# Second attention: the float8 stage's quantised rows transposed by DMA from SBUF to SBUF, in place of TensorE and ScalarE

## The reference

```python
x = x + _L1_xattn_ref(_layernorm(x), ctx_1024, ctx_1024, fside_BxSxS2_0, ...)   # 16 heads of 16, bias fside * lambda
x = x + _L1_ffn_ref(_layernorm(x), L1_ffn_weight, L1_ffn_bias)

def _L1_ffn_ref(x, weight, bias):
    x_mat = quantize_e4m3(x2d, SCALE).astype(jnp.float16)    # clip to 448, round to float8
    w_mat = quantize_e4m3(weight, SCALE).astype(jnp.float16)
    out2d = (x_mat @ w_mat.T).astype(jnp.float32)
    return (out2d + bias)
```

## Time and profile before

| | |
|---|---|
| time, median of 3 runs (lowest, highest) | 1896.82 us (1893.7, 1897.35) |
| profiled execution: its own time, its span | 1893.5 us, 1891.7 us |
| granted TensorE clock, mean over the span | 0.975 of full |
| PE, DVE, ACT, POOL busy over the span | 89%, 63%, 59%, 36% |
| last phase in the span | 1469.9 to 1891.7 us |
| one steady turn of it | 24.7 us |

### The profile page before, as it was taken

How to read it: one execution, slowest core, us unless ns; L and a number is a source line. 1 busy time by engine, 2 the same in 40 slices (tenths; PEclk the granted TensorE clock), 3 DMA queues, 4 the chain that set the end, 5 groups by cost and what they waited for, 6 DMA issues and landing times. The chain is left out here.

```text
span 1891.7 us, 40735 instructions
## 1 busy us (share of the span) xinstructions
PE 1683.7 (89%) x13412; PEld 1382.6 (73%) x13412; DVE 1187.3 (63%) x4106; ACT 1117.7 (59%) x2571; POOL 683.4 (36%) x857
## 2 busy tenths in 40 slices
PE   6777777769999999999997899989999899999995
PEld 5555555557788888888996777777778677777774
DVE  6799999857301101011113899999985798888885
ACT  5599999942222222222334665666664788888894
POOL 4423232321211111110104466656654244445544
PEclk9899999979999999999998999999999899999998
DMA  3100010025855655655985200000000201111110
GB/s 131 49 19 27 19 27 19 3 79 187 274 174 176 201 178 169 202 178 161 332 270 168 73 23 20 15 23 23 23 29 1 74 23 34 35 36 35 36 63 29
DMA packets 111696, 171.96 MB, mean 91 GB/s; under 512 B 6832, under 2 KB 86576, under 8 KB 110864
## 3 DMA queue, kind: packets, MB, share of 16 engines
q1 hardware_dynamic: 95248, 142.55, 23.1%
q0 software_dynamic: 6480, 17.70, 3.2%
q10 hardware_dynamic: 9776, 9.31, 1.4%
HBM read 143.45 MB, written 26.08 MB: 90 GB/s over the span
## 5 line engine op out<-in xcount | busy, mean ns | idle before, releaser
L2151 ACT ACTIVATE moe_hT<-moe_p_h,lane_a 128x256 f32<-128x256 f32 (+1 forms) x344 | 131.4, 433 | 370.7 <-PE moe_p_h L2093 370.7
L2093 PE MATMUL moe_p_h<-moe_gT,moe_w 128*128 128x256 f32 (+1 forms) x1376 | 256.4, 345 | 0.8 <-issue 0.8
L2103 PE MATMUL moe_p_y<-moe_w,moe_hT 128*128 128x256 f32 x1136 | 252.3, 379 | 0.0
L2093 PEld LDWEIGHTS moe_p_h<-moe_gT,moe_w 128*128 128x128 f32 x1376 | 227.8, 192 | 25.8 <-issue 1.2
L1584 ACT ACTIVATE xb_pr<-xb_sc,xb_nmax 128x256 f32<-128x256 f32 x512 | 222.7, 503 | 29.9 <-DVE xb_nmax L1667 28.2
L1983 POOL DMA_INDIRECT moe_gx<-moe_tokens,moe_source_i x71 | 67.4, 949 | 457.5 <-PE moe_p_t L2080 401.5
L2103 PEld LDWEIGHTS moe_p_y<-moe_w,moe_hT 128*128 128x128 f32 x1136 | 212.5, 190 | 27.1
L999 ACT ACTIVATE xa_pr<-xa_sc,xa_nmax 128x256 f32<-128x256 f32 (+1 forms) x512 | 204.0, 452 | 21.3 <-DVE xa_nmax L1079 20.5
L1667 DVE CUSTOM_DVE_ANT_0 xb_sc<-xb_p_s,begun_area 128x256 f32<-128x256 f32 x512 | 187.1, 419 | 41.0 <-PE xb_p_s L1415 39.4
L2271 DVE COPY moe_gT<-moe_p_t 128x512 f32<-128x512 f32 (+1 forms) x43 | 25.7, 599 | 233.2 <-PE moe_p_t L2080 226.8
L2296 DVE TENSOR_TENSOR moe_gy<-moe_p_y,lane_a 128x256 f32<-128x256 f32 x71 | 27.6, 421 | 229.0 <-PE moe_p_y L2103 229.0
(11 more groups left out here) (376 smaller groups left out, 3442.1 us busy)
## 6 DMA issues: line engine op xcount, KB each, us to landing
moe_w<-in_L_ffn_w_dram SPq DMA_DIRECT2D x86, 1024.0 KB
begun_area<-xb_kv SPq DMA_DIRECT2D x32, 256.0 KB, 2.8
moe_rows_out<-moe_gy ACTq DMA_DIRECT2D x28, 256.0 KB
xb_kv<-moe_w SPq DMA_DIRECT2D x18, 256.0 KB, 4.9
X<-in_x_dram SPq DMA_DIRECT2D x4, 1024.0 KB, 9.5
xa_ctx<-in_ctx_turned_dram SPq DMA_DIRECT2D x16, 256.0 KB, 9.8
moe_tokens<-moe_XN_s SPq DMA_DIRECT2D x16, 256.0 KB, 2.3
xb_raw<-in_fside_BxSxS_dram SPq DMA_DIRECT2D x15, 256.0 KB, 3.7
```

Source lines behind the costliest of these rows:

```text
L2093: last = pe.matmul(p_h[n % 3][:, k * width:(k + 1) * width], w1[:, r, ic, (2 * n + k) * P:(2 * n + k + 1) * P], gT[:, r % 2, ic, 0:width], ...
L2103: last = pe.matmul(p_y[:, t * D:(t + 1) * D], hT[:, hc, t * P:(t + 1) * P], w2[:, r, hc, :], start=(hc == 0), stop=(hc == HC - 1))
L2151: last = act.activation(hT[:, 2 * n + k, 0:width], p_h[n % 3][:, k * width:(k + 1) * width], ACT.Gelu, bias=b1[:, bass.ds(e * HC + 2 * n + ...
```

## The change

The bf16 transposes of f_xq leave PE, and the copy of p_a to f_xT leaves ACT. SP issues two DMAs with transpose instead, from f_xq straight to f_xT, one for each tile of 128 rows (64 KB each), in its iteration b for batch b - 2; for batches 14 and 15 after its loop and ahead of the stores. They count on a semaphore of their own, f_xT_in, for which PE's product waits, and for which the writers of the single f_xq wait. The identity's bf16 copy goes, and with it PE's wait for it.

```diff
@@ block.sync
+            def turn_float8(f):
+                sp.wait_ge(s_["f_quantised"], f + 1)
+                if f >= 1:
+                    sp.wait_ge(s_["f_y_ready"], f)
+                for t in range(TB):
+                    sp.dma_start(f_xT[:, :, t * P:(t + 1) * P], f_xq[:, t, :], transpose=True).then_inc(f_xT_in, 16)
+
             for b, h, s in turns(sp):
                 if has_next(b):
...
                     load(b + 1, h + s, 1 - s)
+                if b >= 2:
+                    turn_float8(b - 2)
+            turn_float8(B - 2)
+            turn_float8(B - 1)
             out_v = out.rearrange("b (t p) d -> p (b t) d", p=P)
@@ block.gpsimd
-            pool.tensor_copy(ident_b[:, :], ident[:, :]).then_inc(s_["ident_set"], 1)
...
-                    wait_alone(pool, s_["stood_p"], (s_["f_turned"], f))
+                    wait_alone(pool, s_["stood_p"], (f_xT_in, 16 * TB * f))
@@ block.tensor
-            def turn_float8(f):
-                pe.wait_ge(s_["f_quantised"], f + 1)
-                for c in range(DC):
-                    for t in range(TB):
-                        last = pe.transpose(p_ab[:, c * S + t * P:c * S + (t + 1) * P], f_xq[:, t, c * P:(c + 1) * P], ident_b[:, :])
-                last.then_inc(s_["f_turned"], 1)
...
-                pe.wait_ge(s_["f_x_ready"], f + 1)
+                pe.wait_ge(f_xT_in, 16 * TB * (f + 1))
...
-            pe.wait_ge(s_["ident_set"], 1)
...
-                    if g == 1 and b >= 3:
-                        pe.wait_ge(s_["o_ready"], TB * (b - 1) + 1)
-                        turn_float8(b - 3)
...
                     if g == 1 and b >= 3:
+                        pe.wait_ge(s_["o_ready"], TB * (b - 1) + 1)
                         multiply_float8(b - 3)
...
-                turn_float8(f)
                 multiply_float8(f)
@@ block.scalar
-            def read_float8(f):
-                act.wait_ge(s_["f_turned"], f + 1)
-                if f >= 1:
-                    act.wait_ge(s_["f_y_ready"], f)
-                act.activation(flat(f_xT[:, :, :]), p_ab, ACT.Copy).then_inc(s_["f_x_ready"], 1)
...
-                    if g == 1 and b >= 3:
-                        read_float8(b - 3)
...
-                read_float8(f)
                 read_float8_product(f)
@@ block.vector
-                wait_alone(dve, s_["stood_v"], (s_["f_turned"], f))
+                wait_alone(dve, s_["stood_v"], (f_xT_in, 16 * TB * f))
```

More of the change, by code:

```diff
@@ L1186, in biased_attention_and_float8 @@
         wt_ffn = sh.wt_ffn
-        ident_b = ph.sb("ident_b", [P, P], BF16)
         f_stats = ph.sb("f_stats", [P, TB, 6])
@@ L1215, in biased_attention_and_float8 @@
         p_a = ph.ps("p_a")
-        p_ab = p_a[:, :].bitcast(BF16)[:, 0:512]
         p_s = [ph.ps(f"p_s{i}") for i in range(4)]
@@ L1223, in biased_attention_and_float8 @@
                  "pv sums_read sums_turned o_ready turned_o oT_ready y_ready y_biased added chain_v chain_p stood_v stood_p "
-                 "ident_set f_measured f_var f_rooted f_normed f_cast f_quantised f_turned f_x_ready f_y_ready f_y_read "
+                 "f_measured f_var f_rooted f_normed f_cast f_quantised f_y_ready f_y_read "
                  "f_biased f_added f_last stored").split()
@@ L1228, in biased_attention_and_float8 @@
         raw_in = [ph.sem(f"raw_in{s}") for s in range(2)]
+        f_xT_in = ph.sem("f_xT_in")
         block = ph.block()
```

## The result

| | before | after |
|---|---|---|
| median of six runs each (lowest, highest) | 1895.82 us (1893.49, 1897.35) | 1903.01 us (1900.94, 1906.51) |
| profiled execution: its time, its span | 1893.5, 1891.7 us | 1901.87, 1900.1 us |
| granted clock, mean | 0.975 | 0.972 |

The ratio is 1.0041, 95% interval 1.0027 to 1.0054: slower by 7.2 us between the medians, 5 to 10 by the interval. The place, the sign and the mechanism were as predicted; the loss was forecast at 11.3 us.

What follows compares the result with a forecast made beforehand. Steady turns bound by a path through DVE, ACT, PE, DVE, unaffected; end: 1883.85 + 0.14 + 3.1 + 11.5 + 3.8 + 1.0 - 0.4 = 1903.0 us span, 1904.8 profiled, 1908.1 us for the median, range 1902 to 1920.

Steps and rivals of the forecast that it cites:

- inner range of 1902 to 1912: Own range of the likeliest forecast, 1908.1 us, chance 0.72: bounds of the pair's time and 3.7 us between runs.
- The bound and the hidden work: Steady turns, 24.7 us: path DVE, ACT, PE, DVE; removed 0.40 on PE and 0.60 on ACT lie beside it, gain 0.
- Rivals A and D: Steady turns shorter: first up to 1.0 us each, 1891.8, chance 0.02; second 0.5 to 0.8, 1897 to 1901, 0.06.
- The start: At phase start, without POOL's identity copy and PE's wait for it, first scores come 0.4 us earlier, kept to the end.
- I take 3.1 us: Time the two transposing DMAs of a batch hold SP and its queue; bounds 0.8 to 6.4 us.
- Rivals B and C: Pair holds SP over 12.1 us, turns grow, 1944 at 14, chance 0.10; second 6.4 to 12.1, 1911 to 1917, 0.10.
- The ring and its threshold (12.1 us): Quantise, transposes, loads, POOL keys, quantise: closes in pair time + 3.6 + 8.95 us, so under 12.1 the turn stays 24.7.
- The stores: At the end: all four behind SP's last pair, big store issued 1887.1 not 1810.34, landing 11.5, others 3.8 us more.
- I take 0: PE's four transposes a batch, 0.40 us: removal gains nothing, hidden by two units turned behind; at most 0.40 a turn.

Runs made afterwards that it cites:

- e7: Before without float8 transposes, copies or DMAs in their place; the product reads an f_xT filled once, PE doesn't wait at its first scores: 1892.37 us, one run.
- e3: Before with PE's wait for the identity moved from its first scores to its first float8 transposes: 1898.77 us, one run.
- e1: After with stores earlier in SP's order, batches 0 to 10 ahead of batch 12's pair, 11 and 12 ahead of batch 14's: 1895.42 us, ratio 1.0011 to before.
- e4: e1 with transposes and copies of batches 14 and 15 back on PE and ACT: 1893.74 us, ratio 0.9993.
- e5: e1 with transposes and copies of batches 13 to 15 back on PE and ACT: 1896.74 us, ratio 1.0006.
- e6: After with three or five spare transpose pairs ahead of each true one, batches 0 to 13: 1902.22 us with four pairs, 1964.11 with six, one run each.
- e2: Before, no DMA transposes, with SP waiting for the last quantised rows ahead of its stores: 1904.74 us, ratio 1.0052.

## Why the prediction was right, and where it was off

The forecast was 1908.1 us, range 1902 to 1920, and slower with 0.92; it came out at 1903.0, in the range, near its lower end. Of the 5.1 us between, 1.0 is the base: the median of before was 1896.82 over three runs and 1895.82 over six. The inner range of 1902 to 1912 takes the 3.7 us of the runs' spread off at its lower end and doesn't add it at the upper, which would be 1915; no verdict hangs on that. By its steps:

- **The bound and the hidden work: right for the steady turn.** 24.68 us in after, ACT idle 1.53 us (forecast about 1.5), and turns 0 to 15 take 390.0 to 390.2 us in three profiles of before and three of after alike. e7 shows that even no turning at all leaves it. Rivals A and D fall.
- **The start: right.** First scores 0.04 us behind SP's first issue in after, 0.46 before; e3 shows 0.41 us. In after the first scores also took 1.23 us against 2.09, at a granted clock of 0.86 against 0.50; the other two profiles of after have 2.09 and 1.44, so this is chance in part. Of the other kernels that do not wait for the identity, e1, e3, e4, e5 and e7 had 2.09 and the two of e6 1.50 and 1.91; the four profiles that wait (before three times, e2) all had 2.09.
- **"I take 3.1 us" for the pair: 2.5 measured.** The bounds (0.8, 6.4) held it. The row that I doubled, the longest issue of 1.56 us, was an outlier; one transposing DMA holds SP for 1.24, three times a plain issue of 0.43. Rivals B and C fall. A landing is counted from the start of its issue, so the pair had landed 1.29 + 0.04 + 2.39 = 3.72 us after SP began it, where the prediction set the landing behind the whole hold (3.1 + 2.8 = 5.9); that is 2.2 of the 3.4 us by which the last add came earlier than forecast (1889.67 against 1893.1), off the path in either case. The Trainium skill's 1309 ns for 128 x 128 by DMA ("VectorE: DVE Perf Modes", section "The three transpose paths") would have been 5.2 us for the pair, an estimate. It is twice what SP was held (2.46), and 1.5 more than the 3.72. The Trainium skill's "Advanced Engine Details and Errata", section "X-Bar Transpose (TRN2)", has transposing DMAs as fast as regular ones. The trace agrees for the landing, 2.4 us for 64 KB against 3.0 for the 256 KB loads of the same stretch (the 192 KB between them are 0.6 us at 346 GB/s), not for the issue.
- **The ring and its threshold (12.1 us): right in kind.** e6 with about 11 us shows no longer turn, with 16.2 us one of 29.1 where the rule gives 28.8. Where between 11 and 16.2 it starts wasn't measured.
- **The stores: right.** All four behind the last pair, in one block to the end; e2 makes 6.8 of E's 9.6 us without any transposing DMA, e1 takes it away. The block was forecast at 11.5 + 3.8 + 1.0 = 16.3 us and took 14.87. The step that failed is setting the other stores' 3.8 us of bytes behind the big store's landing of 11.5. In before that store had the DMA queue to itself (the last load was issued at 1782.08), and its bytes ran at full rate only from 1811.3 to 1819.8; the last 2 us before the landing moved almost nothing. In a block the next store's bytes fill that time: in after the bytes run without a gap from 1886.3 to 1898.5. 2816 + 1280 KB at 346 GB/s are 12.1 us, and the rest, 2.8, is the delay to the first bytes and the end.
- **"I take 0" for PE's transposes, "in turns 3 to 16 and twice in the tail": wrong in turn 16.** The cover named, two units turned behind them, exists in turns 3 to 15 only; in turn 16 there are no scores and no units left, PE works from wait to wait, and transposes, copy and product are in series (1868.04 - 1866.96 = 1.08 us). I had read one steady turn and carried its answer to the last.
- **The clock.** With PE's work in turn 16 broken by those waits, D averages 23.3 us over six profiles, without 21.8 over five. The means for before and after alone are 23.6 and 21.7.

The terms against L, three profiles each, means 424.2 and 430.9, +6.7: E gives 17.5 - 7.9 = +9.6 (forecast 11.7: pair 0.6 and block 1.4 less), D gives -1.9 (forecast 0), and SP's first issue to the first shift gives -0.9 (2.63 and 1.70 on the mean; forecast -0.4). That is +6.8, and the medians differ by 7.2. The forecast was right on E within 2.1 us by its mechanism; what D gave was in no term of it, and part of what the start gave is luck of the clock. In D, turn 16 is 1.08 us shorter by the float8 work itself (9.70 against 10.78 where its sums are fast); how much of that reaches the end, and what a clock that falls earlier adds beside it, isn't separated: what the clock does differs between executions of one kernel, and eleven profiles with two kinds of kernels are too few to call it shown.

No version beat before beyond its interval. e4, with the stores early, the last two batches on PE and all others by DMA, stood at 0.9993 [0.9979, 1.0007].

## What to carry to other kernels

A step moved onto a queue that issues in order is charged at the queue's end too: what stands behind it there (here 4 MB of stores that had been free) costs more than the step (about 7 us against the pair's 2.5), and sending the stores ahead of the last pairs gave 7.3 of E's 9.6 us back (e1). Work that hides in a steady turn must be looked up again in the last turn, where the cover is gone. For the length of a block of stores that runs alone take bytes over the full rate plus the delay around it (2.8 us here); the landing of a single store holds an end in which few bytes move, and the next store's bytes run there.

## What was unexpected of the hardware

- A DMA with transpose from SBUF to SBUF (128 x 256 bf16, 64 KB) held SP for 1.17 to 1.37 us (median 1.24) and landed 2.4 us after the start of its issue, in 32 of them; in rows of ten (e6) the mean was 1.31 to 1.41, with single ones up to 2.54.
- The same instructions of one kernel ran at either clock level from one execution to the next after a few short waits: the last output product took 1.99, 3.78 and 3.78 us in before and 3.78, 3.66 and 1.99 in after.
- A store of 2816 KB landed in 9.9 to 10.1 us in the six profiles with three stores right behind it (after three times, e2, e6 twice), and in 10.5 to 11.5 in the five where it had the queue to itself (before three times, e3, e7); with three loads of 256 KB just ahead of it 11.1 to 11.8 (e1, e4, e5). Why it is slower without stores behind it isn't shown.
